# Two rows of numbers that VectorE compares with are read from a PSUM bank in place of SBUF, in a graph network's sorts and first layer

## The reference

```
h = relu(layernorm(x))
# first layer: for every edge, a weighted row of h is added to a node, both ways
x_fwd[src] += w * h[dst, :128];  x_bwd[dst] += w * h[src, 128:]     # then divided by the counts
x = x + concat(x_fwd / deg_src, x_bwd / deg_dst)
h = relu(layernorm(x))
# second layer: eight attention heads of 64, then one output head of 256
z = h @ W.T + b
e = exp(-leaky_relu((z @ a1)[src] + (z @ a2)[dst], 0.2))
z' = segment_sum(e * z[dst], src);  z' = elu(layernorm(z') * g + beta)
x = x + elu(second pass of the same kind, of width 256)
```

## Time and profile before

| | us |
|---|---|
| median of 3 runs | 3130.86 |
| lowest, highest | 3130.0, 3134.51 |
| the profiled execution | 3138.38 |
| its span | 3136.6 |
| granted TensorE clock, mean | 0.849 of full speed |

### The profile page before, as it was taken

How to read it: one execution, slowest core, us unless ns; L and a number is a source line. 1 busy time by engine, 2 the same in 40 slices (tenths; PEclk the granted TensorE clock), 3 DMA queues, 4 the chain that set the end, 5 groups by cost and what they waited for, 6 DMA issues and landing times. The chain is left out here.

```text
span 3136.6 us, 48973 instructions
## 1 busy us (share of the span) xinstructions
PE 2368.6 (76%) x16450; PEld 1814.2 (58%) x16450; DVE 2162.2 (69%) x4446; ACT 1589.7 (51%) x4526; POOL 2049.6 (65%) x2003
## 2 busy tenths in 40 slices
PE   1777689888898789875667788888884677777761
PEld 1677688878888688853334444444443555555551
DVE  9999888878887698843226588888877433434337
ACT  0454466656665566643333445545547555555544
POOL 1010277777777777777774577777766477777772
PEclk7999899989999799975558899999996887887775
DMA  2001011111112411122226577777780233333352
GB/s 63 1 1 43 16 46 45 45 47 47 46 47 46 49 45 45 44 58 51 51 52 82 175 209 209 210 208 210 208 181 8 74 107 105 106 106 106 106 96 57
DMA packets 114891, 270.64 MB, mean 86 GB/s; under 512 B 34543, under 2 KB 51670, under 8 KB 114646
## 3 DMA queue, kind: packets, MB, share of 16 engines
q0 software_dynamic: 89088, 245.53, 31.4%
q1 hardware_dynamic: 25558, 21.98, 2.1%
HBM read 250.96 MB, written 16.42 MB: 85 GB/s over the span
## 5 line engine op out<-in xcount | busy, mean ns | idle before, releaser
L388 POOL DMA_INDIRECT rows_near<-table_a,s_idx_S x464 | 534.8, 1153 | 227.5 <-issue 112.5
L1039 DVE TENSOR_TENSOR work<-work,bank 128x129 f32 (+2 forms) x928 | 390.4, 421 | 302.9 <-PE bank L725 208.7
L388 POOL DMA_INDIRECT rows_near<-table_b,s_idx_D x464 | 500.0, 1078 | 141.4 <-issue 105.4
L388 POOL DMA_INDIRECT rows_near<-table,s_idx_S x464 | 446.7, 963 | 173.6 <-issue 124.3
L388 POOL DMA_INDIRECT given<-table,s_idx_S x464 | 448.0, 965 | 141.3 <-issue 124.6
L725 PE MATMUL bank<-rows_near,oh 128*128 128x129 f32 x1856 | 385.3, 341 | 180.8 <-ACT rows_near L497 146.9
L711 PE MATMUL bank<-scratch 128*128 128x224 bf16 (+1 forms) x2520 | 401.7, 270 | 110.2 <-DVE scratch L1014 77.4
L841 PE MATMUL bank<-scratch,oh 128*128 128x512 f32 x928 | 448.7, 629 | 21.3 <-DVE scratch L1197 21.3
L711 PE MATMUL bank<-rows_near,sort_ring 128*128 128x224 bf16 (+1 forms) x2520 | 403.0, 271 | 68.4 <-ACT sort_ring L488 39.8
L725 PEld LDWEIGHTS bank<-rows_near,oh 128*128 128x128 f32 x1856 | 295.2, 227 | 258.4 <-ACT rows_near L497 189.8
L580 ACT ACTIVATE e_att<-lrelu 128x32 f32<-128x32 f32 (+1 forms) x232 | 50.4, 217 | 606.0 <-DVE lrelu L1186 606.0
(11 more groups left out here) (198 smaller groups left out, 4431.3 us busy)
## 6 DMA issues: line engine op xcount, KB each, us to landing
rows_near<-table_a,s_idx_S POOLq DMA_INDIRECT x464, 2.7
rows_near<-table_b,s_idx_D POOLq DMA_INDIRECT x464, 2.7
rows_near<-table,s_idx_S POOLq DMA_INDIRECT x464, 3.6
given<-table,s_idx_S POOLq DMA_INDIRECT x464, 3.6
table<-scratch SPq DMA_DIRECT2D x25, 260.0 KB, 2.1
table<-scratch SPq DMA_DIRECT2D x25, 128.5 KB, 2.9
xs<-in_x SPq DMA_DIRECT2D x1, 3072.0 KB
out_x<-scratch SPq DMA_DIRECT2D x24, 128.0 KB, 1.7
```

What stands on the lines that cost most here:

```text
L388: nc.gpsimd.indirect_dma_start(out=to, out_offset=None, in_=table[:, :], in_offset=bass.IndirectOffsetOnAxis(ap=s_idx[order][:, c:c + 1], ...
L1039: v.tensor_add(a, a, psum).then_inc(sum_free[o], 1)
```

## The change

One tensor `pairs_made` in SBUF takes the casts of lane and chunk numbers, packed as 16-bit pairs in 4-byte words. Before the first batch, VectorE copies 128 words of `iota_f` and the 296 words of `pairs_made` into bank 3, where `iota_sum`, `iota_lane` and `iota_chunk` now lie; ahead of the copies it waits for `w_evac`. L1008, L1009 read their first input there in all four parts, and L1031 in all of phase S and in phase D up to step 102; from `FIRST` on it reads `iota_f` as before, since the dense part writes bank 3. The second inputs, the outputs, the sizes and the types are as they were, and so are L1013, L1014 and L1039.

```diff
         iota_f = sb("iota_f", [P, 512])
-        iota_lane = sb("iota_lane", [P, P], BF16)
-        iota_chunk = sb("iota_chunk", [P, CHUNKS], FP16)
+        pairs_made = sb("pairs_made", [P, (P + CHUNKS) // 2])
+        iota_sum, pairs_kept = bank[3][:, 0:P], bank[3][:, P:P + (P + CHUNKS) // 2]
+        iota_lane, iota_chunk = pairs_kept[:, 0:P // 2].bitcast(BF16), pairs_kept[:, P // 2:].bitcast(FP16)
...
-            v.tensor_copy(iota_lane[:, :], iota_i[:, 0:P])
-            v.tensor_copy(iota_chunk[:, :], iota_i[:, 0:CHUNKS])
+            v.tensor_copy(pairs_made[:, 0:P // 2].bitcast(BF16), iota_i[:, 0:P])
+            v.tensor_copy(pairs_made[:, P // 2:].bitcast(FP16), iota_i[:, 0:CHUNKS])
...
                 v.tensor_tensor(oh[:, q * QUAD % SLOTS:q * QUAD % SLOTS + QUAD, :],
-                                iota_f[:, 0:P].unsqueeze(1).to_broadcast([P, QUAD, P]),
+                                (iota_f[:, 0:P] if phase and q >= FIRST else iota_sum).unsqueeze(1).to_broadcast([P, QUAD, P]),
...
             dve.wait_ge(fields_made, 1)
+            dve.wait_ge(w_evac, 1)
+            v.tensor_copy(iota_sum, iota_f[:, 0:P])
+            link(v.tensor_copy(pairs_kept, pairs_made[:, :]))
```

## The result

| | before | changed | ratio |
|---|---|---|---|
| median, us | 3130.47 (4 runs) | 3048.74 (4 runs, 3047.27 to 3054.22) | 0.9739 (0.9725 to 0.9752) |
| again, beside other runs of before | 3131.16 (7 runs) | 3050.25 (4 runs, 3047.36 to 3053.23) | 0.9739 (0.9721 to 0.9757) |

Forecast were 3067 us, 64 us less; measured are 82 less. The sign, the mechanism and the order of the parts held; the gain was 18 us larger.

The account below looks back on a forecast made before the run. GpSimd's gather issue was taken to bound the first layer, VectorE the first sort. Stretches 60 plus phase D's later steps 5 minus copies 1 made 64 us, so 3131 became 3067 us; own range 3041 to 3101, for all 3041 to 3134.

Parts of the forecast that it names:

- GpSimd's issue paces the first layer: Phase S and the rest of phase D: 208 gathers x 0.30 plus 246.9 busy make 309.3 of 310 us.
- Two inputs in SBUF hold a gather, a bank as one of them does not: Gathers starting during VectorE instructions: held with two SBUF inputs, 1.36 us; not held with one input in PSUM, 0.94.
- The replay: Gather starts worked through a batch step: 4 gathers in 6.25 us become 9 in 12.5; 24 to 26 us less per stretch.
- Neither engine can close up fully, so of the 24 us I take 20: First-layer stretches: VectorE and TensorE wait for each other in turn, so each stretch gains 20 us, bounds 10 and 30.
- Three stretches at 20: The three first-layer stretches of 52 steps with a sort beside gathers: 20 us less each, 60 us together.
- Steps 52 to 102 of phase D: L1031 reading the bank there shortens the 254 gathers: 5 us less, between 0 and 10.
- First sort and copies: First sort's comparisons keep their duration, 0 us; two added copies ahead of it cost some 0.8 us, bounds 0.5 to 1.5.
- The first: Rival: a bank input puts 16-bit comparisons at the 32-bit pace, in first sort and stretches; 213 us more, 3344; 15 in 100.
- The second: Rival: the comparisons' second input, still in SBUF, holds the gathers, so nothing is freed; 3131 to 3132 us; 9 in 100.
- TensorE didn't take over: Rival that TensorE sets the stretches' pace: only 10 of 24 us each come, 3097 us; no chance of its own.
- The range: Forecast's own range for the whole kernel, 3041 to 3101 us, from 10 and 30 us a stretch; forecast 76 in 100.
- The marks I had set: Phase S: no gather over 1.3 to 1.5 us, mean 1.05 to 1.10, some 40 us shorter; VectorE and TensorE above 0.92 busy.

Follow-up runs that it names:

- r2: Against the kernel before, only the chunk-number comparison reads the bank, lane comparison and one-hots reading SBUF: 3063.7 us, ratio 0.9785 beside before at 3131.16.
- e6: Changed kernel, but the first layer gathers only each phase's first 16 chunks and every fourth after: 3045.1 us, ratio 0.8839 beside before at 3444.29.
- r1: The changed kernel run once more, unaltered: 3050.25 us, ratio 0.9739 beside the kernel before at 3131.16.
- e3: Changed kernel with copies and packed tensor kept, but all comparisons reading SBUF: 3439.62 us, ratio 0.9997 beside before at 3439.49.

## Why the prediction was right, point by point

**GpSimd's issue paces the first layer: shown at 3131 us.** The gaps are 0.305 us before and after, so GpSimd never waits for a slot, and the stretches shrink by what the gathers shrink: 208 x (1.190 - 1.061) = 26.8 us, which is the first stretch's whole gain. Where something else paces the layer (3440 us), the same shorter gathers bring nothing.

**Two inputs in SBUF hold a gather, a bank as one of them does not: shown**, by counts of 0 against all in one kernel (r2).

**The replay: right in the step after, rough in its base.** It gave 26 us a stretch by its own base, 24 by the trace's, against 26.8, 20.3 and 27.7 measured. "The very times of the earlier trace rows" holds for three of them (3.26, 4.73, 6.21); the first gather of the rows starts at 1.10 and not at 1.21, which changes nothing, as it is held to the same end. The prediction also took 310 us for all three stretches; the second took 302.0, with the narrower comparison, and so it had least to give.

**"Neither engine can close up fully, so of the 24 us I take 20": wrong, and most of the error.** I had read L1008's 34.4 us of waits for TensorE as something between these two engines. They fell to 12.3 us in the changed kernel, where more work was to be done in less time:

```profile
L1009 DVE TENSOR_TENSOR scratch<-bank,given 128x1280 bf16<-128x1280 bf16 x21 | 17.2, 818 | 6.0 <-PE bank L714 6.0
...
L1009 DVE TENSOR_TENSOR sort_ring<-bank,given 128x1280 bf16<-128x1280 bf16 x20 | 16.4, 819 | 6.3 <-PE bank L714 6.3
```

TensorE had been late because ScalarE was, and ScalarE because the rows were issued slowly (277 us of waits for table A's rows over phase S before, 224 after). The waits come in lumps: 32 of the 34.4 us are eight waits of 3.5 to 5.3 us. I had overlooked what stands some 7 us ahead of seven of them: TensorE stops for 2.5 us until ScalarE's sixth field (L488) is there, and is then granted the lower of its two clock levels. Ahead of the wait of 3.77 us at 602.02 it is:

```profile
595.07 0.76 PE L711 MATMUL bank<-rows_near,sort_ring 128*128 128x240 bf16 x3 [2.52 <-ACT sort_ring L488]
```

```profile
564.00:595.00 31.00, 25.75 (x240) 24.11 (x240) 28.46 (x43) 20.04 (x66) 24.77 (x21) 1.00 0.17 46
595.10:598.40 3.30, 3.30 (x17) 2.43 (x18) 2.99 (x6) 1.21 (x5) 2.62 (x3) 0.50 0.13 40
```

The clock falls from 1.00 to 0.50, and three matmuls of L711 take 0.80 us there and 0.47 behind it. There are nine such stops in the first stretch. Seven are followed by half clock and by a wait of VectorE of 3.5 to 4.0 us; the other two (469.86 and 565.38) are followed by neither. From the first batch of a part to its last TensorE is at half clock for 38.2, 49.2 and 23.9 us before and for 22.4, 26.1 and 11.6 in the changed kernel. So faster gathers gave back some of TensorE's clock as well. That this order of events is cause and effect is read from the rows; no run holds the clock fixed. It also fits that the second part of the changed kernel (281.2 us, 26.1 at half clock) stays 17 us above e6's (264.4, 6.8 at half clock), which was not tested either.

Three stretches at 20 made 60 us; measured are 74.8. Of these 15 us, out of 18 in all, the discount is 12, and 3 are the base of 24.

**Steps 52 to 102 of phase D:** 5 us taken, 6.7 measured. r2, without the one-hots in the bank, keeps 3.2 of them by the position of its gathers, so a little over half (4.1 us between r1 and r2) belongs to L1032.

**First sort and copies:** the comparisons there take 815 and 1312 ns, 820 and 1320 to 1340 before, so 0 was right. The first gather comes 1.3 us later, 0.8 was taken; but in r1 and r2 it comes at 363.1 and 363.6, so this is within what two profiles differ. `w_evac` was long there.

**The rivals.** The first (16-bit comparisons at the 32-bit pace, 15 in 100) fell with the first row of the groups. Its price per comparison was right, its bill for the stretches untested. The second fell with the counts above. TensorE didn't take over: 20 to 28 us a stretch came, not 10.

**The range.** 3041 to 3101 counts the stretches alone (30 and 10 us each) and leaves out the prediction's own terms for L1031 and the copies; 3049 lies near its lower end, inside it either way.

**The marks I had set:** no gather longer than 1.3 to 1.5 us was nearly met (5 of 928 are longer, the longest 1.60; before it was 107, up to 2.18). The mean is 1.061 in the first stretch and 1.038 over the rest of phase S (1.05 to 1.10 said), and phase S is 48 us shorter (40 said). VectorE is busy for 0.91 to 0.93 of the three stretches and TensorE for 0.89 to 0.94; so "both at 96%" was too high, and they had more room than I thought.

## What to carry to other kernels

Lay the rows of two engines beside each other before trusting a mean: a GpSimd gather of 1.19 us was 0.94 of work and 0.25 of standing behind VectorE, and the cure was to move one constant operand. When two periodic engines hold each other, replay the starts over one or two periods: which instruction is freed counts for more than how long it is (one of three comparisons, half of the time, gave five sixths of the gain). And before taking a discount for "the next engine", ask who causes that engine's waits: those that come from the bottleneck go with it, and TensorE's clock can come back with them.

## What the runs showed of the hardware that I had not expected

- The hold is exact. A held gather ends 0.817 us behind the end of the VectorE instruction that holds it (in the changed kernel 262 of 266 within 0.005), and at 603.12 it cost 0.92 us. VectorE shows no trace of it.
- A bank as input costs a two-input comparison nothing, at 16 bits (815 against 820 ns for 1280 elements, 1397 against 1400 for 2400) and at 32 (682 and 682 for 512). The Trainium skill's table in "VectorE: DVE Perf Modes" ("The perf-mode tier table") would have had 1x for the 16-bit ones; the measurement goes with the Trainium skill's "Vector Engine (DVE) Microarchitecture Reference", section 5.1.
- In the first stretch before, seven of nine stops of TensorE of 2.5 us were followed by some 3.3 us at half its clock (0.50), and only these seven by a long wait of VectorE.
- The same kernel took 3131 us in two groups of runs and 3440 in three, with 209 and 166 GB/s in the second layer, and in the slower groups TensorE stopped 146 times (70 us) in e3's first layer ahead of matmuls that wait for no semaphore. The chunk row alone gained 2.1% in the one and 0.0% in the other.
